# Moving VectorE's first convolution products ahead of the second tile's D folds

## The chip, the cores and the metric

The kernel runs on one core of one Trainium2 chip. The metric is the device time of one execution in microseconds, lower is better. TensorE, VectorE (DVE in the rows), ScalarE (ACT) and GpSimd (POOL) each work through their own list of instructions in order and meet at semaphores. Most loads and all transpositions by DMA are issued by SyncE (SP), in order too.

## The reference

Two layers of a gated block on x (8 x 256 x 512) with a context of the same shape. Only the first mixing step matters here:

```python
# layer 0: k = v = context, q = layernorm(x); 32 heads of 8 rows, L = 512
kv = einsum('bhil,bhjl->bijhl', k_, v_)
y = irfft(rfft(kv, 2L) * rfft(ssm_kernel, 2L))[..., :L]     # a causal convolution along l
out = y + kv * D[None, None, None, :, None]
out = einsum('bijhl,bhil->bjhl', out, q_)
x = x + tanh(g_xattn[0]) * out
# then: a ternary feed forward (hidden 1408), attention to the context with a mask,
# a 1-bit feed forward (hidden 2048) with activations quantised in groups of 64
```

## The kernel before

The convolution is done as matmuls. A tile n (NT = 16 of them) holds two heads, for all 8 batches: 128 rows of x. For each head (hh = 0, 1) the taps stand in SBUF as Toeplitz blocks, `toep[n % 2]`, 4 blocks of 128x128, loaded with an overlapping access pattern. D is folded into the taps: adding D to the tap of delay 0 adds kv * D to the convolution. The products of pairs of context rows (36 per batch and head, `kv[n % 2]`) are the moving operand; they are made by GpSimd (`pairs(n)`, three multiplications of 128x512 and one of 128x256) and ScalarE (`square(n)`). Half a tile is 10 products of blocks (`conv_part`, each recorded as two matmuls of 128x288), with results in 4 of the 8 banks of PSUM: banks 0 to 3 for hh = 0, banks 4 to 7 for hh = 1.

Per tile the engines do this.

- VectorE: `ln_sums(dve, 0, n)` (bn_stats and bn_aggr of x tile n); `products(n, hh)`, four instructions (lines 1253, 1255, 1257, 1262) that multiply the convolution's result by q and free its banks (`s_prod`); `fold_heads(n, hh)` (line 1268).
- GpSimd: `pairs(n + 1)`, `ln_root` and `conv_offset` (the reciprocal deviation and the offset from the sums), `finish_heads`, `add_result`.
- ScalarE: `join_q(n + 1)`, `square(n + 1)`, `norm_q(n + 2)` (line 1026, normalises x), `split_q(n + 2)` (line 992, parts the result into two 16-bit planes), from n = 2 `copy_result(n - 2)` (line 1033), and then pieces of the weights of the next stage.
- SP: for each n, loads of x and context and weights, then `turn_q_planes(n + 2)` (line 371, a DMA transposition of the planes, which waits for split_q), then `load_toeplitz(n + 2)` (line 359). `join_q` (line 1003) waits for the transposition to land.
- TensorE: `conv(n)`: half 0, then from n = 2 `turn_result(n - 2)` into bank 5, then half 1 in the order of blocks lo = 2, 3, 0, 1; ahead of lo = 1, which writes bank 5, it waits for `copy_result(n - 2)`.

The first tiles are special. Tile 0's and tile 1's Toeplitz blocks come straight from the input without D, and VectorE adds D on the diagonal (`fold_first_d`, line 1451, four instructions in all). Those of tiles 2 to 15 come from `kpad`, a copy of the taps in memory: VectorE adds D to the taps (line 1479, 32x1 elements), and SP then stores them (line 456). Tiles 0 and 1 of q are turned by TensorE (`turn_q`) and copied by ScalarE (`copy_q`, lines 981 and 983), the later ones by DMA. `s_first` counts the first pairs (2) and the four folds; fold_first_d(0, 1), the fourth count, comes before everything that the change touches.

In the kernel before VectorE's list begins so: first pairs, fold (0, 0), sums of x tile 0, fold (0, 1), sums of x tile 1, and then the part that the change moves. Line 1479 is the taps' add:

```python
                dve.wait_ge(s_tp[1], 16)
                fold_first_d(1, 0)
                fold_first_d(1, 1)
                dve.wait_ge(s_kin, 32)
                nc.vector.tensor_tensor(kp_sb[:, P - 1:P], kp_sb[:, P - 1:P], d_sb[:, :], ALU.add).then_inc(s_dadd, 1)
                dve.wait_ge(s_xl[2], 16)
                ln_sums(dve, 0, 2)
                for n in range(NT):
                    products(n, 0)
```

Of the kernel before, what the change touches and what calls it, by code (L numbers as in the profile page):

```python
# [5 lines left out]
ALU = mybir.AluOpType  # L6
# [8 lines left out]
P = 128  # L15
# [9 lines left out]
def at(v, off, dims):  # L25
    return bass.AP(v.tensor, v.offset + off, [v.ap[0]] + dims)


def flamingo_two_layers(nc, xc, cx, ctxt_in, ctx_in, mask, g_xattn, g_ffn, taps_in, dskip, a_w, b_w, out):
# [30 lines left out]
    with ExitStack() as ctx:  # L60
        def sb(name, shape, dt=F32):
            return ctx.enter_context(nc.sbuf_tensor(name, shape, dt))

        def sem(name):
            return ctx.enter_context(nc.semaphore(name))
# [20 lines left out]
        d_sb = sb("d_sb", [H, 1])  # L86
# [14 lines left out]
        def view(off, shape, dt=F32):  # L101
            n = 1
            for s in shape:
                n *= s
            words = n if dt == F32 else n // 2
            v = arena[:, off:off + words]
            if dt != F32:
                v = v.bitcast(dt)
            if len(shape) == 1:
                return v  # L110
            names = "abcd"[:len(shape)]
            return v.rearrange(f"p ({' '.join(names)}) -> p {' '.join(names)}", **dict(zip(names, shape)))
# [3 lines left out]
        kp_sb = view(R_A, [TAP])[0:H, :]  # L116
# [53 lines left out]
        def bank(i):  # L170
            return psum[:, i, :]
# [10 lines left out]
        s_kin = sem("taps_and_d_loaded")  # L182
        s_dadd = sem("d_folded")
        s_tfirst = sem("first_toeplitz_and_d_loaded")
        s_first = sem("first_pairs_and_d_added")
# [3 lines left out]
        s_xl = [sem(f"x_loaded{i}") for i in range(NT)]  # L189
        s_cx = [sem(f"context_loaded{i}") for i in range(2)]  # L190
        s_tp = [sem(f"toeplitz_loaded{i}") for i in range(2)]
# [87 lines left out]
        def ln_sums(dve, stage, n):  # L279
            nc.vector.bn_stats(ln_bn[:, stage, n % 2, :], x_sb[:, n, :]).then_inc(s_ln[stage], 1)  # L280
            dve.wait_ge(s_ln[stage], 2 * n + 1)
            nc.vector.bn_aggr(ln_ag[:, stage, n, :], ln_bn[:, stage, n % 2, :]).then_inc(s_ln[stage], 1)
# [56 lines left out]
        with nc.Block() as block:  # L339
# [371 lines left out]
            def _(pe):  # L711
# [6 lines left out]
                def turn_result(n, to, freed):  # L718
                    pe.wait_ge(s_res, 2 * n + 2)
                    pe.wait_ge(s_prod, freed)  # L720
                    for lb in range(LB):
                        last = nc.tensor.transpose(bank4(to)[:, lb, :], res[n % 3][:, lb, :], ident[:, :])  # L722
                    last.then_inc(s_rt, 1)
# [6 lines left out]
                def conv_block(n, hh, lo):  # L730
                    for li in range(lo + 1):
                        last = conv_part(n, hh, lo, li)
                    return last
# [33 lines left out]
                def conv(n):  # L767
                    pe.wait_ge(s_kv, n + 2)
                    pe.wait_ge(s_sq, n + 2)
                    if n == 1:  # L770
                        pe.wait_ge(s_first, 6)
                    else:
                        pe.wait_ge(s_tp[n % 2], 16 * (n // 2 + 1))
                    pe.wait_ge(s_prod, 2 * n - 1)
                    for lo in CONV_ORDER:
                        last = conv_block(n, 0, lo)
                    last.then_inc(s_y, 1)
                    pe.wait_ge(s_prod, 2 * n)
                    if n >= 2:
                        turn_result(n - 2, 5, 2 * n)  # L780
                    if n in TOT_STEP:
                        w = TOT_STEP[n]
                        pe.wait_ge(s_red, w + 1)
                        nc.tensor.matmul(bank(4)[:, w:w + 1], ones[:, :], tot[:, w:w + 1], start=True, stop=True
                                         ).then_inc(s_tot, 1)
                    for lo in CONV_ORDER:
                        if n in TOT_STEP and lo == 0:
                            pe.wait_ge(s_mean, 2 * TOT_STEP[n] + 1)
                        if n >= 2 and lo == 1:
                            pe.wait_ge(s_re, n - 1)  # L790
                        last = conv_block(n, 1, lo)
                    last.then_inc(s_y, 1)
# [450 lines left out]
            def _(dve):  # L1243
                def products(n, hh):
                    dve.wait_ge(s_y, 2 * n + hh + 1)
                    dve.wait_ge(s_qc, n + 1)
                    if n >= 2:
                        dve.wait_ge(s_res, 2 * n - 3 + hh)
                    y = psum[:, 4 * hh:4 * hh + 4, :].rearrange("p l c -> p (l c)")
                    q = q_ext[n % 3][:, hh, :]  # L1250
                    pr = prod[n % 2][hh]
                    rows = LB * B
                    nc.vector.tensor_tensor(at(pr, 0, [[SLOTS, rows], [E, 4], [1, E]]), at(y, 0, [[64, rows], [1, 32]]),  # L1253
                                            at(q, 0, [[EX, rows], [1, 4], [1, E]]), ALU.mult)
                    nc.vector.tensor_tensor(at(y, NP, [[64, rows], [E, 3], [1, E]]), at(y, E, [[64, rows], [E, 3], [1, E]]),
                                            at(q, 0, [[EX, rows], [0, 3], [1, E]]), ALU.mult)
                    nc.vector.tensor_tensor(at(pr, 32, [[SLOTS, rows], [4, 2], [1, 4]]),
                                            at(y, 32, [[64, rows], [0, 2], [1, 4]]),
                                            at(q, 4, [[EX, rows], [4, 2], [1, 4]]), ALU.mult).then_inc(s_fold, 1)
                    dve.wait_ge(s_fold, 2 * n + hh + 1)  # L1260
                    side = at(pr, 1, [[SLOTS, rows], [9, 3], [1, E]])
                    nc.vector.tensor_tensor(side, side, at(y, NP, [[64, rows], [E, 3], [1, E]]), ALU.add).then_inc(s_prod, 1)  # L1262
# [8 lines left out]
                def a_weight_mean(w):  # L1271
                    dve.wait_ge(s_tot, w + 1)
                    nc.vector.tensor_scalar(a_mean[:, w:w + 1], bank(4)[:, w:w + 1], 1.0 / (FA * L), TINY,
                                            ALU.mult, ALU.max).then_inc(s_mean, 1)
# [174 lines left out]
                def fold_first_d(n, hh):  # L1449
                    diag = toep[n][:, hh, 0:P]  # L1450
                    nc.vector.scalar_tensor_tensor(diag, at(ident[:, :], P - 1, [[-1, P]]),
                                                   d_first[:, n * G + hh:n * G + hh + 1], diag, ALU.mult, ALU.add
                                                   ).then_inc(s_first, 1)
# [18 lines left out]
                fold_first_d(0, 1)  # L1472
                dve.wait_ge(s_xl[1], 16)
                ln_sums(dve, 0, 1)
                dve.wait_ge(s_tp[1], 16)
                fold_first_d(1, 0)
                fold_first_d(1, 1)
                dve.wait_ge(s_kin, 32)
                nc.vector.tensor_tensor(kp_sb[:, P - 1:P], kp_sb[:, P - 1:P], d_sb[:, :], ALU.add).then_inc(s_dadd, 1)
                dve.wait_ge(s_xl[2], 16)  # L1480
                ln_sums(dve, 0, 2)
                for n in range(NT):
                    products(n, 0)
                    if n in TOT_STEP:
                        a_weight_mean(TOT_STEP[n])
                    fold_heads(n, 0)
                    if n in TOT_STEP:
                        w = TOT_STEP[n]
                        dve.wait_ge(s_mean, 2 * w + 1)
                        nc.vector.reciprocal(a_inv[:, w:w + 1], a_mean[:, w:w + 1]).then_inc(s_mean, 1)  # L1490
                    if n + 3 < NT:
                        dve.wait_ge(s_xl[n + 3], 16)
                        ln_sums(dve, 0, n + 3)
                    products(n, 1)
                    if NT - 3 <= n < NT - 1:
                        a_scale_x(n + 3 - NT)
                    if NT - 4 <= n < NT - 1:
                        a_stats(n + 4 - NT)
                    if n == max(TOT_STEP) + 1:
                        dve.wait_ge(s_tanh, 1)  # L1500
                        nc.vector.tensor_tensor(a_down[:, :], a_mean[:, 2:3], gates[:, 2:3], ALU.mult).then_inc(s_tanh, 1)
                    if n + 1 in TOT_STEP:
                        w = TOT_STEP[n + 1]
                        dve.wait_ge(s_wa, 4 * w + 4)
                        nc.vector.tensor_reduce(tot[:, w:w + 1], a_abs[:, w, :], AX.X, ALU.add).then_inc(s_red, 1)
                    if n < NT - 1:
                        fold_heads(n, 1)
# [170 lines left out]
```

## Time and profile before

| | |
|---|---|
| median of 3 runs | 692.79 us (692.38 to 692.96) |
| the profiled execution | 692.67 us |
| its span | 690.8 us |
| TensorE busy | 682.7 us, 99% of the span |
| VectorE busy | 581.0 us, 84% |
| ScalarE busy | 410.3 us, 59% |
| GpSimd busy | 294.7 us, 43% |
| mean granted TensorE clock | 0.998 |

The span is the stretch from the first to the last instruction of the profiled execution; the execution's own time is 1.9 us longer. The times in rows count from the start of the span. An engine's busy share is a mean over all stages; the convolution takes the first 171 us of the span.

### The profile page before, as it was taken

How to read it: one execution, taken by the hardware profiler on the slowest of the kernel's cores; microseconds unless marked ns; L12 is line 12 of the kernel's file. 1: busy time of each engine (PE TensorE's matmuls, PEld its weight loads, DVE VectorE, ACT ScalarE, POOL GpSimd, SP SyncE). 2: the span in 40 equal slices, each digit the busy share in tenths (PEclk: the TensorE clock that was granted, in tenths of full speed). 3: DMA queues.
4: the chain of work that ended last, by engine and by line, in shares of the span. 5: the costliest groups of instructions: out<-in, count | busy, mean ns of one | idle time of the engine just before them, and what ended most of it. 6: DMA issues, size and time to landing. Idle time of an engine off the chain costs nothing.

```text
span 690.8 us, 9572 instructions
## 1 busy us (share of the span) xinstructions
PE 682.7 (99%) x3162; PEld 389.0 (56%) x3162; DVE 581.0 (84%) x1054; ACT 410.3 (59%) x630; POOL 294.7 (43%) x455
## 2 busy tenths in 40 slices
PE   9999999999999999999999999999999999999997
PEld 7777777777444444577744444444444444444445
DVE  5998999999998998658957889988898888898891
ACT  3689898857779898657677344423434423434440
POOL 6799999999755554537401431111110011110000
PEclk9999999999999999999999999999999999999999
DMA  8995674653478789897040243353332233342244
GB/s 297 243 299 187 220 194 131 154 150 102 127 159 194 180 179 205 226 360 277 19 134 17 61 107 77 76 93 92 76 92 39 68 92 92 78 77 61 62 69 114
DMA packets 155376, 94.64 MB, mean 137 GB/s; under 512 B 133824, under 2 KB 134336, under 8 KB 155328
## 3 DMA queue, kind: packets, MB, share of 16 engines
q1 hardware_dynamic: 153600, 90.02, 51.4%
q0 software_dynamic: 1200, 3.93, 1.7%
q8 instruction: 25, 0.41, 0.3%
q14 instruction: 23, 0.19, 0.1%
q10 hardware_dynamic: 528, 0.09, 0.1%
HBM read 53.04 MB, written 8.47 MB: 89 GB/s over the span
## 4 chain that ended last, share of the span: by engine, by line
PE 87%; DVE 6%; POOL 3%; DMA 2%; ACT 1%; issue 1%; SPq 0%; POOLq 0%
PE psum L877 29%; PE psum L726 16%; PE psum L909 15%; PE psum L804 11%; PE psum L816 5%; PE psum L860 4%; PE psum L838 4%; DMA phase_space<-in_taps 1%; PE psum L893 1%; PE psum L827 1%; POOL phase_space L576 1%; PE psum L722 1%; DVE phase_space L1253 1%; DVE phase_space L1426 1%; DVE phase_space L1359 1%
## 5 line engine op out<-in xcount | busy, mean ns | idle before, releaser
L877 PE MATMUL psum<-phase_space 128*128 128x512 f16 x1024 | 223.8, 379 | 0.1
L877 PEld LDWEIGHTS psum<-phase_space 128*128 128x128 f16 x1024 | 99.9, 98 | 122.3 <-issue 1.7
L726 PE MATMUL psum<-phase_space 128*128 128x288 f32 x640 | 158.8, 407 | 1.4 <-DVE phase_space L1262 1.4
L726 PEld LDWEIGHTS psum<-phase_space 128*128 128x128 f32 x640 | 120.4, 191 | 33.6 <-issue 1.8
L705 POOL DMA_DIRECT2D out<-x_sb x15 | 9.3, 620 | 234.7 <-DVE x_sb L1435 234.7
L909 PE MATMUL psum<-phase_space 128*128 128x512 f16 x480 | 105.7, 379 | 0.0
L1200 ACT ACTIVATE phase_space<-psum,b_scalars 128x512 f32<-128x512 f32 x64 | 43.4, 681 | 75.3 <-PE psum L877 75.2
L1206 ACT ACTIVATE phase_space<-phase_space,magic 128x1024 f32<-128x1024 f32 x32 | 36.5, 1148 | 77.3 <-DVE phase_space L1419 77.3
L804 PE MATMUL psum<-phase_space 128*128 128x512 bf16 (+1 forms) x384 | 78.9, 362 | 0.2 <-DVE phase_space L1262 0.2
L909 PEld LDWEIGHTS psum<-phase_space 128*128 128x128 f16 x480 | 46.9, 98 | 56.7
L1404 DVE SCALAR_TENSOR_TENSOR phase_space<-psum,b_scalars,phase_space 128x512 f32<-128x512 f32 x64 | 47.7, 748 | 28.5 <-ACT phase_space L1200 28.4
L804 PEld LDWEIGHTS psum<-phase_space 128*128 128x128 bf16 x384 | 37.4, 98 | 40.2 <-DVE phase_space L1262 0.7
L576 POOL TENSOR_TENSOR phase_space<-phase_space 128x512 f32<-128x512 f32 x45 | 52.4, 1190 | 0.0
L1359 DVE TENSOR_REDUCE phase_space<-phase_space 128x8 f32<-128x512 f32 (+1 forms) x32 | 47.4, 1480 | 0.5
L280 DVE BATCH_NORM_STATS2 ln_bn<-x_sb 128x6 f32<-128x512 f32 x64 | 43.5, 679 | 2.1 <-DMA x_sb<-x_between 1.7
L1253 DVE TENSOR_TENSOR phase_space<-psum,phase_space 128x1024 f32<-128x1024 f32 x32 | 39.1, 1221 | 6.6 <-PE psum L726 6.4
L300 POOL TENSOR_SCALAR phase_space<-x_sb,ln_nm,ln_rs 128x512 f32<-128x512 f32 x48 | 37.8, 788 | 13.1 <-POOL ln_rs L295 6.0
L816 PE MATMUL psum<-phase_space 128*128 128x512 bf16 x176 | 40.6, 379 | 0.9 <-issue 0.6
L1066 ACT ACTIVATE phase_space<-psum,a_scalars 128x512 f32<-128x512 f32 (+1 forms) x48 | 30.8, 642 | 14.1 <-PE psum L804 13.1
L307 POOL TENSOR_TENSOR phase_space<-phase_space 128x512 f16<-128x512 f32 x12 | 13.8, 1179 | 59.4 <-ACT phase_space L1212 59.4
L1426 DVE SCALAR_TENSOR_TENSOR phase_space<-phase_space 128x1024 f32<-128x1024 f32 x32 | 37.8, 1224 | 1.3
L1301 DVE SCALAR_TENSOR_TENSOR phase_space<-psum,a_scalars,phase_space 128x512 f32<-128x512 f32 (+1 forms) x48 | 33.2, 697 | 5.9 <-ACT phase_space L1066 4.9
(123 smaller groups left out, 1070.9 us busy)
## 6 DMA issues: line engine op xcount, KB each, us to landing
phase_space<-in_L_weights SPq DMA_DIRECT2D x24, 512.0 KB, 6.0
phase_space<-in_L_weights SPq DMA_DIRECT2D x12, 704.0 KB, 7.2
phase_space<-kpad SPq DMA_DIRECT2D x14, 512.0 KB, 4.3
phase_space<-in_context_heads SPq DMA_DIRECT2D x15, 384.0 KB, 5.0
x_sb<-in_x_tiles SPq DMA_DIRECT2D x16, 256.0 KB, 4.8
phase_space<-in_context_turned SPq DMA_DIRECT2D x8, 512.0 KB, 5.9
x_between<-x_sb SPq DMA_DIRECT2D x16, 256.0 KB
x_sb<-x_between SPq DMA_DIRECT2D x16, 256.0 KB, 7.0
```

Source lines behind the costliest of these rows:

```text
L280: nc.vector.bn_stats(ln_bn[:, stage, n % 2, :], x_sb[:, n, :]).then_inc(s_ln[stage], 1)
L576: nc.gpsimd.tensor_tensor(at(kv_k, d * E, [[NP, rows], [1, E]]), at(cx_sb[k], 0, [[EX, rows], [1, E]]), at(cx_sb[k], d, [[EX, rows], [1, E ...
L726: return nc.tensor.matmul(at(bank(4 * hh + lo), 0, [[64, B], [1, NP]]), toep[n % 2][:, hh, (lo - li) * P:(lo - li + 1) * P], kv[n % 2][:, ...
L804: last = nc.tensor.matmul(bank(UPA[c][part])[:, 0:w], fa_qT[t % 4][:, kk, :], a_wT[part][:, kk, c0:c0 + w], start=(kk == 0), stop=(kk == L ...
L816: last = nc.tensor.matmul(bank(6 + t % 2), fa_hT[t % 2][:, c, :], a_wT[2][:, c, :], start=(c == 0), stop=(c == JA - 1))
L877: last = nc.tensor.matmul(bank(2 * (m % 3) + w), fb_qT[n % 2][:, kk % 2, kk // 2, :], b_wT[w][:, kk // 2, c * 512:(c + 1) * 512], start=(k ...
L909: last = nc.tensor.matmul(bank(6 + k), fb_hT[k][:, part, c, :], b_wT[2][:, c, :], start=(c == 0 and part == 0), stop=(c == JB - 1 and part ...
L1200: nc.scalar.activation(fb_s[m % 2], bank(2 * (m % 3)), ACT.Silu, scale=fb_sm[:, n % 4, 2:3]).then_inc(g_si, 1)
L1253: nc.vector.tensor_tensor(at(pr, 0, [[SLOTS, rows], [E, 4], [1, E]]), at(y, 0, [[64, rows], [1, 32]]), at(q, 0, [[EX, rows], [1, 4], [1, E ...
L1359: nc.vector.tensor_reduce(gx[:, 0, :], grouped(src), AX.X, ALU.max, apply_absolute_value=True).then_inc(s_steps, 1)
L1404: nc.vector.scalar_tensor_tensor(fb_h[n % 2][:, c * 512:(c + 1) * 512], bank(2 * (m % 3) + 1), fb_sm[:, n % 4, 3:4], fb_s[m % 2], ALU.mult ...
L1426: nc.vector.scalar_tensor_tensor(grouped(fb_t[k][:, cols]), grouped(fb_t[k][:, cols]), MAGIC, spread(fb_gh[k][:, 3, gr], NGH // 2), ALU.su ...
```

## The change

VectorE's products(0, 0) are put ahead of the two folds of tile 1, the taps' add and the sums of x tile 2. TensorE's wait for the folds of tile 1 is split: half 0 waits for the fifth count of s_first, half 1 for the sixth.

```diff
@@ conv(n), TensorE
                     if n == 1:
-                        pe.wait_ge(s_first, 6)
+                        pe.wait_ge(s_first, 5)
                     else:
                         pe.wait_ge(s_tp[n % 2], 16 * (n // 2 + 1))
                     pe.wait_ge(s_prod, 2 * n - 1)
@@
                     last.then_inc(s_y, 1)
                     pe.wait_ge(s_prod, 2 * n)
+                    if n == 1:
+                        pe.wait_ge(s_first, 6)
                     if n >= 2:
                         turn_result(n - 2, 5, 2 * n)
@@ VectorE
                 ln_sums(dve, 0, 1)
-                dve.wait_ge(s_tp[1], 16)
-                fold_first_d(1, 0)
-                fold_first_d(1, 1)
-                dve.wait_ge(s_kin, 32)
-                nc.vector.tensor_tensor(kp_sb[:, P - 1:P], kp_sb[:, P - 1:P], d_sb[:, :], ALU.add).then_inc(s_dadd, 1)
-                dve.wait_ge(s_xl[2], 16)
-                ln_sums(dve, 0, 2)
                 for n in range(NT):
                     products(n, 0)
+                    if n == 0:
+                        dve.wait_ge(s_tp[1], 16)
+                        fold_first_d(1, 0)
+                        fold_first_d(1, 1)
+                        dve.wait_ge(s_kin, 32)
+                        nc.vector.tensor_tensor(kp_sb[:, P - 1:P], kp_sb[:, P - 1:P], d_sb[:, :], ALU.add).then_inc(s_dadd, 1)
+                        dve.wait_ge(s_xl[2], 16)
+                        ln_sums(dve, 0, 2)
```

## Rows read from the trace of the kernel before

**Rows 1.** The page's head and its first part: busy us, share, instructions

```profile
span 690.8 us, 9572 instructions
PE 682.7 (99%) x3162; PEld 389.0 (56%) x3162; DVE 581.0 (84%) x1054; ACT 410.3 (59%) x630; POOL 294.7 (43%) x455
```

**Rows 2.** TensorE's waits: line waited for, total us, times, longest us

```profile
PE psum L726 <- DVE phase_space L1262: 1.4, 1, 1.4
...
PE psum L816 <- issue: 0.6, 1, 0.6
```

**Rows 3.** The chain that ended last, first 75 us: start us, us, what

```profile
11.41 1.72 DVE phase_space L1451 x2
...
18.39 14.79 PE psum L726 x60
...
33.62 9.90 PE psum L726 x40
...
54.31 9.70 PE psum L726 x40
```

**Rows 4.** TensorE's timeline, end of tile 0: start us, us, what

```profile
13.92 3.08 PE L726 MATMUL psum<-phase_space 128*128 128x288 f32 x12
```

**Rows 5.** VectorE's timeline, 8 to 24 us

```profile
8.23 0.32 DVE L1451 SCALAR_TENSOR_TENSOR phase_space<-ident,d_first,phase_space 128x128 f32<-128x128 f32 x1
...
13.05 1.06 DVE L1479 TENSOR_TENSOR phase_space<-phase_space,d_sb 32x1 f32<-32x1 f32 x1
14.05 0.67 DVE L280 BATCH_NORM_STATS2 ln_bn<-x_sb 128x6 f32<-128x512 f32 x1
...
14.86 1.21 DVE L1253 TENSOR_TENSOR phase_space<-psum,phase_space 128x1024 f32<-128x1024 f32 x1
...
17.29 0.95 DVE L1262 TENSOR_TENSOR phase_space<-phase_space,psum 128x768 f32<-128x768 f32 x1
18.28 0.69 DVE L1268 TENSOR_TENSOR phase_space<-phase_space 128x512 f32<-128x512 f32 x1
...
19.71 1.20 DVE L1253 TENSOR_TENSOR phase_space<-psum,phase_space 128x1024 f32<-128x1024 f32 x1
...
22.14 0.95 DVE L1262 TENSOR_TENSOR phase_space<-phase_space,psum 128x768 f32<-128x768 f32 x1
```

**Rows 6.** GpSimd's timeline: pairs(1)

```profile
10.90 3.21 POOL L576 TENSOR_TENSOR phase_space<-phase_space 128x512 f32<-128x512 f32 x3
```

**Rows 7.** ScalarE's timeline, 12 to 45 us

```profile
12.24 0.38 ACT L983 ACTIVATE phase_space<-psum 128x256 f32<-128x256 f32 x1
...
16.25 0.81 ACT L1026 ACTIVATE phase_space<-x_sb,ln_off,ln_rs 128x512 f32<-128x512 f32 x1 [0.74 <-POOL ln_off L584]
...
23.21 2.10 ACT L1003 ACTIVATE phase_space<-phase_space 128x512 uint16<-128x512 uint16 x4 [4.87 <-DMA phase_space<-phase_space]
...
36.71 0.67 ACT L1033 ACTIVATE phase_space<-psum,gates 128x512 f32<-128x512 f32 x1
...
40.52 2.08 ACT L1003 ACTIVATE phase_space<-phase_space 128x512 uint16<-128x512 uint16 x4 [0.42 <-DMA phase_space<-phase_space]
...
44.86 0.67 ACT L1033 ACTIVATE phase_space<-psum,gates 128x512 f32<-128x512 f32 x1
```

**Rows 8.** SyncE's queue, 18 to 28 us

```profile
18.31 1.35 SPq L371 DMA_TRANSPOSE phase_space<-phase_space  x1
19.77 1.83 SPq L359 DMA_DIRECT2D phase_space<-kpad  x1
...
27.72 1.24 SPq L371 DMA_TRANSPOSE phase_space<-phase_space  x1
```

**Rows 9.** DMA issues from 19 to 21 us: KB each, median us to landing

```profile
phase_space<-kpad SPq DMA_DIRECT2D x1, 512.0 KB, 6.2
phase_space<-phase_space SPq DMA_TRANSPOSE x1, 4.8
```

**Rows 10.** TensorE's weight loads, 30 to 48 us

```profile
37.42 5.63 PEld L726 LDWEIGHTS psum<-phase_space 128*128 128x128 f32 x24 [0.38 <-ACT phase_space L1033]
```

**Rows 11.** Windows: us, busy (instructions) by engine, granted clock, DMA share, GB/s

```profile
17.30:18.40 1.10, 0.01 (x1) 0.04 (x1) 1.07 (x2) 1.04 (x3) 0.00 (x0) 1.00 0.03 12
...
685.00:690.80 5.80, 1.45 (x14) 1.05 (x11) 0.48 (x1) 0.00 (x0) 0.00 (x0) 0.81 0.07 23
```

## The prediction

> **What bounds the kernel now.** I read the page's head first: the span is 690.8 us and TensorE is busy for 682.7 us of it [rows 1]. So almost any time that the kernel could gain is a gap on TensorE, and any new gap there is lost for good unless a later gap takes it up. The waits of TensorE say where the gaps are: one of 1.4 us, released by VectorE's line 1262, is the only one of more than 1 us once the convolution has begun [rows 2]. The chain of work that ended last leads through it. In time order it has the two folds of D into tile 1's Toeplitz blocks at 11.41, and further on 60 matmuls that start at 18.39 and run without a break for 14.79 us [rows 3]. TensorE's own timeline gives the gap's left edge: the last 12 matmuls of tile 0 start at 13.92 and end near 17.0 [rows 4]. TensorE then idles until 18.39 for products(0, 0), which frees banks 0 to 3.
>
> VectorE's timeline shows why these products are late. Their four instructions run from 14.86 to 18.24 (17.29 + 0.95) [rows 5]. Ahead of them stand the folds, the taps' add at 13.05, which takes 1.06 us for 32x1 elements, and the sums of x tile 2 at 14.05. The short jobs are long because GpSimd's pairs(1) run beside them, three multiplications from 10.90 to 14.11 [rows 6]: the add ends just as they do, while a fold with GpSimd at small jobs took 0.32 us at 8.23 [rows 5]. The products' inputs are there earlier. The last part of copy_q(0) on ScalarE ends at 12.24 + 0.38 = 12.62 [rows 7], and the first half of tile 0's convolution is done before that.
>
> **What the change moves.** No operation is added or removed. Four products (3.38 us) pass ahead of two folds, the taps' add with its store on SP's queue, and ln_sums(0, 2). TensorE's wait for six counts of s_first becomes five, with the sixth ahead of tile 1's second half.
>
> First the intended side. Products(0, 0) start at about 12.7 instead of 14.86 and end at 12.7 + 3.38 = 16.1. Fold(1, 0) ends at 16.1 + 0.05 + 0.32, about 16.45. Both are ahead of 17.0, where TensorE is free, so the 1.39 us gap goes and tile 1 starts near 16.95.
>
> Next, what is late. VectorE now does the folds, 0.3 us each in sequence, from 16.15 to 16.75. The uncontended taps' add has no row: it lies between nothing and the 1.06 us seen beside GpSimd [rows 5]. GpSimd has finished pairs(1) by then and waits for the very sums that follow, so I take 0.1 us. The bn_stats of x tile 2 then start at 16.8 instead of 14.05: late by **2.75 us**. By the ends (products at 12.62, both folds in 0.5, add at nothing: 16.5; everything as I take it and the add at 1.06: 17.75) it is 2.45 to 3.7 us. The rule for these short jobs is in the Trainium skill, "SBUF — State Buffer", section "SBUF: two separate sides": VectorE with two SBUF inputs and GpSimd take one port pair in turn, each for a whole instruction. By it the add costs nothing extra once GpSimd is idle, and by the 1.06 us of the row it would cost 0.96 us more; the add's end at GpSimd's end agrees with the rule.
>
> VectorE's next job for TensorE is late too. The sums of tile 2 took 0.81 us from start to next start (14.05 to 14.86), and from fold_heads(0, 0) at 18.28 over the sums of tile 3 to products(0, 1) at 19.71 it was 1.43 us [rows 5]. So products(0, 1) start at 16.8 + 0.81 + 1.43 = 19.05 and end 3.38 later at 22.45. TensorE reaches that point at 16.95 + 4.93 = 21.9 (a half tile is 20 of the 60 matmuls, 14.79 / 3) [rows 3]. So 0.7 us come back as a wait there: tile 1's second half starts at about 22.6 (0.15 after the products, as at 18.39) instead of 18.39 + 4.93 = 23.3, a lead of 0.7 us.
>
> Now who waits for x tile 2. The queue is GpSimd (rstd and offset), then ScalarE's norm_q(2) at 16.25 and split_q(2), then on SP the transposition of its planes at 18.31, and behind it in the same queue the Toeplitz load of tile 2 at 19.77 [rows 7, 8]. Norm_q(2) waited for that input (0.74 us idle). SP has nothing to do meanwhile, and the DMA engines are nearly idle then (share 0.03 from 17.3 to 18.4 [rows 11]), so each of these moves by the full 2.75 us. The kpad store moves from 14.14 by about as much and lands before it is wanted. The Toeplitz load took 6.2 us to land and the transposition 4.8 [rows 9]. The load lands at 19.77 + 6.2 + 2.75 = 28.7. TensorE wants it at 22.6 + 4.93 = 27.5 and starts tile 2 at about 28.8 instead of 28.25, after a wait of 1.3 us: already 0.55 us behind the kernel before.
>
> The decisive one is further along. ScalarE's join_q(2) at 23.21 sat idle for 4.87 us until the transposition landed, and everything ScalarE does afterwards is in order behind it: square(2), norm_q(3), split_q(3). SP's transposition of tile 3 at 27.72 waits for that split; join_q(3) waits for it to land; square(3), norm_q(4), split_q(4) and copy_result(0) at 36.71 follow without a pause [rows 7, 8]. This is a rigid chain: nowhere in it is TensorE waited for. TensorE needs copy_result(0) before block lo = 1 of tile 2's second half, since that frees bank 5. It had to wait for it in the kernel before already: the weight load at 37.42 sat 0.38 us, released by L1033 [rows 10], and the 40 matmuls there took 9.90 us instead of the 9.70 of a later tile [rows 3]. There is no slack left in front of this point. With the chain late by 2.75, the weight load comes at 37.42 + 2.75 = 40.2. Only the 0.55 us of these 2.75, and the 0.2 us of the old wait, are already there when TensorE arrives, so the new gap is 2.75 - 0.55 + 0.2 = 2.4 us, and it swallows lead and lag alike.
>
> From there on the stream of TensorE is solid, and all other engines are late by the same amount, so that their distances to it are as before. (The next copy_result, at 44.86, was limited by its own chain with over 2 us in hand before TensorE wanted it, about 47.9, and keeps them; join_q(4) at 40.52 idled 0.42 us for its transfer.) [rows 7] No large wait later on is there to absorb the shift.
>
> **The sum.** -1.4 (gap at 17.0) + 0.7 (wait for products(0, 1)) + 1.3 (wait for tile 2's Toeplitz blocks) + 2.4 - 0.2 (the wait for copy_result(0), new less old) = 2.8: but for rounding, the end is late by the 2.75 us of x tile 2. The profiled execution took 692.67 us, of which 690.8 are span; with 2.75 that is 695.4. The median before is 692.79, 0.12 above, which gives **695.5 us**, 0.4% slower. A measurement of this kernel tells about 0.2% (1.4 us) from no change.
>
> **Rivals.** *A, the gap is simply saved* (the other side): TensorE starts tile 1 1.39 us earlier and keeps that: 691.4 us. It needs the three later gates to have over 1.4 us in hand. For it speaks that the gap is the only large one; against it that products(0, 1) ended at 22.14 + 0.95 = 23.09 [rows 5], only 0.2 us before TensorE wanted them, and copy_result(0) after that. It decides if copy_result(0) starts at 36.71 - 1.4 = 35.3 or earlier. Chance 0.07.
>
> *B, VectorE's next product is the only limit:* a lead of 0.7 us is kept, 692.1 us. It needs x tile 2 to be late by nothing that matters. *C, the Toeplitz load limits and copy_result(0) does not* (a faster transfer takes up two microseconds of ScalarE's chain): 0.55 us, 693.3 us. For both speaks that ScalarE has idle time: 4.87 us ahead of join_q(2). Against both, this idle time is spent waiting for the late transfer itself. Together 0.15.
>
> *D, the clock.* TensorE's granted clock stayed at 1.00 (2.4 GHz) over the 1.1 us that hold the old gap, while the 5.8 us that hold the idle end show 0.81, a mean of the two levels [rows 11]. The new gap of 2.4 us is longer than the old one, with two of 0.7 and 1.3 us ahead of it. If the clock fell to 1.2 GHz for the half tile behind it, this would take twice its 4.93 us: 695.5 + 4.9 = 700.4 us. The Trainium skill, "TensorE: Matmul & The Clock Gate", section "Part 1: The HAM clock gate", says that an idle TensorE drops to the half rate; that the idle end shows a lower clock agrees. Chance 0.04, since the old gap did nothing.
>
> **How the numbers follow.** The forecast case has 0.74, with its own range 695.1 to 696.5 from the ends 2.45 and 3.7 above. A range from 692.6 to 696.4 takes in C and most of the forecast and leaves out A, D and nearly all of B. Faster by over 0.2%: A and a small part of B, 0.09. Within 0.2%: B and C, 0.14. Slower: forecast and D, 0.77.
>
> **What the profile after should show.** Right: L1253 starting near 12.7, the four products done at 16.1; folds of 0.32 us; no gap at 17.0; TensorE waiting for L1262 until about 22.6; the transposition at 21.1 and the Toeplitz load at 22.5 on SP; join_q(2) at 26.0; copy_result(0) at 39.4 with TensorE waiting about 2.4 us for it. Wrong, if the transposition lands much faster than in 4.8 us, if copy_result(0) comes before 38, or if the shift at 54 us is not the shift at the end.

## The result, and the profile after

The changed kernel takes 694.21 us (median of 18 runs), the kernel before 692.74 (18 runs): a ratio of 1.0024, with a 95% interval from 1.0018 to 1.0031. It is slower, by 1.5 us where 2.75 were forecast. Its 18 executions fall in two groups: 14 took 693.82 to 694.64 us, four took 695.62 to 695.91; the 18 of the kernel before lie between 692.38 and 693.21. One execution of all those in this document, of the experiment e9, ran at a mean granted clock of 0.851 and took 797.66 us; it is left out. In the changed kernel products(n, hh) are lines 1255 to 1264 and fold_heads is line 1270; copy_q is at 983 and 985, norm_q at 1028, join_q at 1005 and copy_result at 1035. Times of a row can differ by up to half a microsecond between executions of one kernel: the folds of tile 1, which wait for the load of their taps, started at 11.41 in one execution of the kernel before and at 11.77 in another (e8).

TensorE's waits in the profile after, to be set against [rows 2]:

```profile
PE psum L726 <- ACT phase_space L1035: 1.8, 1, 1.8
...
PE psum L726 <- DVE phase_space L1264: 0.4, 1, 0.4
```

The wait of 1.4 us for VectorE has become 0.4, and there is a new one of 1.8 us for copy_result(0). VectorE's timeline, which answers to [rows 5], shows the intended side:

```profile
12.71 1.22 DVE L1255 TENSOR_TENSOR phase_space<-psum,phase_space 128x1024 f32<-128x1024 f32 x1 [3.11 <-ACT phase_space L985]
...
15.17 0.95 DVE L1264 TENSOR_TENSOR phase_space<-phase_space,psum 128x768 f32<-128x768 f32 x1
16.04 0.61 DVE L1453 SCALAR_TENSOR_TENSOR phase_space<-ident,d_first,phase_space 128x128 f32<-128x128 f32 x2
16.56 0.14 DVE L1484 TENSOR_TENSOR phase_space<-phase_space,d_sb 32x1 f32<-32x1 f32 x1
16.63 0.68 DVE L280 BATCH_NORM_STATS2 ln_bn<-x_sb 128x6 f32<-128x512 f32 x1
...
21.27 0.95 DVE L1264 TENSOR_TENSOR phase_space<-phase_space,psum 128x768 f32<-128x768 f32 x1
```

The first products start as soon as copy_q(0) has ended and are done at 16.12. The two folds take 0.61 us together and the taps' add 0.14, against 1.72 [rows 3] and 1.06 [rows 5] beside GpSimd's pairs(1). The sums of x tile 2 start at 16.63 instead of 14.05, and products(0, 1) end at 22.22.

What hangs on x tile 2, on GpSimd, on ScalarE (to [rows 7]) and in SyncE's queue (to [rows 8]):

```profile
17.61 0.54 POOL L289 TENSOR_SCALAR ln_ve<-ln_ag 128x1 f32<-128x1 f32 x1 [2.92 <-DVE ln_ag L282]
```

```profile
19.19 0.81 ACT L1028 ACTIVATE phase_space<-x_sb,ln_off,ln_rs 128x512 f32<-128x512 f32 x1 [3.68 <-POOL ln_off L584]
...
24.23 2.09 ACT L1005 ACTIVATE phase_space<-phase_space 128x512 uint16<-128x512 uint16 x4 [2.96 <-DMA phase_space<-phase_space]
...
37.96 0.67 ACT L1035 ACTIVATE phase_space<-psum,gates 128x512 f32<-128x512 f32 x1
```

```profile
21.24 1.36 SPq L371 DMA_TRANSPOSE phase_space<-phase_space  x1
22.71 0.51 SPq L359 DMA_DIRECT2D phase_space<-kpad  x1
...
28.73 1.24 SPq L371 DMA_TRANSPOSE phase_space<-phase_space  x1
```

Norm_q(2) is 2.94 us late, the transposition 2.93. But join_q(2) is late by 1.02 only. The DMA view of these two issues, to [rows 9], has the reason (median us from issue to landing at the end of the row):

```profile
phase_space<-kpad SPq DMA_DIRECT2D x1, 512.0 KB, 4.5
phase_space<-phase_space SPq DMA_TRANSPOSE x1, 2.9
```

The transposition landed in 2.9 us instead of 4.8, the Toeplitz load in 4.5 instead of 6.2. From there the chain goes on as rigidly as forecast: copy_result(0) is 1.25 us late. TensorE's weight loads show the three places where it waits:

```profile
22.28 4.66 PEld L726 LDWEIGHTS psum<-phase_space 128*128 128x128 f32 x20 [0.89 <-DVE phase_space L1264]
27.47 4.66 PEld L726 LDWEIGHTS psum<-phase_space 128*128 128x128 f32 x20 [0.54 <-issue]
...
38.68 5.63 PEld L726 LDWEIGHTS psum<-phase_space 128*128 128x128 f32 x24 [2.22 <-ACT phase_space L1035]
```

The first two waits are short: 0.4 us for products(0, 1), and 0.54 us between weight loads at 27.47, right after the Toeplitz load landed at 22.71 + 4.5 = 27.2. The last row answers to [rows 10]: 38.68 instead of 37.42, 1.26 us late. Up to there TensorE was ahead (its turn_result(0) started at 32.43, before at 33.02). From there on it is behind by what the chain is late, to the end: the span is 692.1 us, 1.3 more. The clock stayed up over the new gap (stretch and its length, then busy us and instructions of TensorE, its weight loads, VectorE, ScalarE and GpSimd, then the granted clock, 1.00 in both, the DMA share and GB/s):

```profile
36.50:38.70 2.20, 0.44 (x3) 0.02 (x1) 1.05 (x3) 2.17 (x5) 1.68 (x4) 1.00 0.99 415
38.70:44.60 5.90, 5.90 (x24) 4.59 (x25) 4.17 (x6) 5.89 (x10) 5.82 (x7) 1.00 0.90 248
```

### The profile page after: what moved, and what is told of

Read it like the earlier page. It is cut to its first block, busy times and chain, and to the rows that moved or that the text cites. A ratio compares the mean times of both kernels' runs of the same rounds, so it can differ in the third digit from the quotient of the medians.

```text
span 692.1 us, 9573 instructions
## 1 busy us (share of the span) xinstructions
PE 683.1 (99%) x3162; PEld 388.7 (56%) x3162; DVE 578.4 (84%) x1054; ACT 410.4 (59%) x630; POOL 295.1 (43%) x455
## 4 chain that ended last, share of the span: by engine, by line
PE 84%; DVE 5%; POOL 3%; ACT 2%; issue 1%; DMA 1%; POOLq 0%; ACTq 0%
PE psum L879 29%; PE psum L911 15%; PE psum L726 14%; PE psum L806 11%; PE psum L818 5%; PE psum L862 4%; PE psum L840 4%; PE psum L895 1%; PE psum L829 1%; POOL phase_space L576 1%; PE psum L722 1%; DVE phase_space L1428 1%; DVE phase_space L1361 1%; DVE phase_space L1255 1%; DMA phase_space<-phase_space 1%
## 5 line engine op out<-in xcount | busy, mean ns | idle before, releaser
L726 PEld LDWEIGHTS psum<-phase_space 128*128 128x128 f32 x640 | 120.0, 190 | 35.3 <-ACT phase_space L1035 2.2
```

Source lines behind the costliest of these rows:

```text
L726: return nc.tensor.matmul(at(bank(4 * hh + lo), 0, [[64, B], [1, NP]]), toep[n % 2][:, hh, (lo - li) * P:(lo - li + 1) * P], kv[n % 2][:, ...
```

## The experiments

Three theories were put against each other. Theory 1: the loss is x tile 2's chain, which ends at copy_result(0). Theory 2: it is the late taps' add with the kpad store and the Toeplitz load behind it. Theory 3: it is the new order of VectorE and TensorE itself.

**Sums of x tile 2 first.** On the changed kernel:

```diff
                 ln_sums(dve, 0, 1)
+                dve.wait_ge(s_xl[2], 16)
+                ln_sums(dve, 0, 2)
                 for n in range(NT):
                     products(n, 0)
...
-                        dve.wait_ge(s_xl[2], 16)
-                        ln_sums(dve, 0, 2)
```

> The changed kernel, but the sums of x tile 2 stand ahead of products(0, 0), where VectorE idled for 3.1 us; the two folds and the taps' add stay behind the products. Theory 1 (the loss is x tile 2's chain, which ends at copy_result(0)): norm_q(2) is back near 16.0, the Toeplitz load and copy_result(0) are back at or before their times in the kernel before (36.7), the loss of 1.5 us is gone. If the transposition lands in 4.8 us the time is 692.5 to 692.8 (TensorE still waits for copy_result(0)), if it lands in 2.9 us the wait is gone too and 691.2 to 691.6 remains. Theory 2 (the loss comes from the late folds, taps' add and kpad store, and the Toeplitz load behind them): the time stays at 694.2. Theory 3 (VectorE's later products are the limit): products(0, 1) end at about 21.4 instead of 22.2, 0.8 us are gained, 693.4.

Measured: 691.94 us, ratio 0.9989 to the kernel before (0.9980 to 0.9998). The whole loss is gone and a gain of 0.8 us is there, with folds, taps' add and kpad store as late as in the changed kernel (store at 17.13, there at 16.73). So these are not the loss. The Toeplitz load, the other half of theory 2, is early again here (20.21), as it stands behind the transposition in SyncE's queue; it is settled by e3 below. The rows of e1 on VectorE, ScalarE and TensorE's weight loads:

```profile
12.31 0.69 DVE L280 BATCH_NORM_STATS2 ln_bn<-x_sb 128x6 f32<-128x512 f32 x1 [2.44 <-DMA x_sb<-in_x_tiles]
```

```profile
16.32 0.81 ACT L1028 ACTIVATE phase_space<-x_sb,ln_off,ln_rs 128x512 f32<-128x512 f32 x1 [0.69 <-POOL ln_off L584]
...
21.54 2.10 ACT L1005 ACTIVATE phase_space<-phase_space 128x512 uint16<-128x512 uint16 x4 [3.13 <-DMA phase_space<-phase_space]
...
35.48 0.67 ACT L1035 ACTIVATE phase_space<-psum,gates 128x512 f32<-128x512 f32 x1
```

```profile
36.20 5.63 PEld L726 LDWEIGHTS psum<-phase_space 128*128 128x128 f32 x24 [0.48 <-ACT phase_space L1035]
```

The transposition landed in 3.1 us here, so the chain was 1.2 us earlier at copy_result(0) than in the kernel before, and TensorE still waited for it. The gain is what the chain allowed, not the 1.4 us of the gap. (The profiled execution, 691.58 us, was the fastest of the 11.) One thing was not seen ahead: x tile 2 had only landed at 12.31, so the sums pushed the products to 13.14.

**The sums late, all else as before.** On the kernel before:

```diff
                 nc.vector.tensor_tensor(kp_sb[:, P - 1:P], ...).then_inc(s_dadd, 1)
-                dve.wait_ge(s_xl[2], 16)
-                ln_sums(dve, 0, 2)
                 for n in range(NT):
                     products(n, 0)
+                    if n == 0:
+                        dve.wait_ge(s_xl[2], 16)
+                        ln_sums(dve, 0, 2)
```

> The kernel before, with the sums of x tile 2 alone moved behind products(0, 0); folds and taps' add stay where they were. Theory 1: products(0, 0) run from 14.1 to 17.45, the gap on TensorE shrinks to 0.65 us, the sums start at 17.5, 3.4 us later than before, and norm_q(2) near 19.9 instead of 16.25. With a transposition that lands in 4.8 us the time is 692.7 + 3.5 = 696.2, with 2.9 us 694.4. Theory 2 (late folds and taps' add cost the time): no loss, the 0.8 us of the gap are gained, 691.9.

Measured: 695.07 us, ratio 1.0034 (1.0021 to 1.0046). It is slower than the changed kernel, though taps' add and kpad store are where they were (store at 14.25). Norm_q(2) starts at 20.02, the transposition lands in 2.9 us and copy_result(0) starts at 38.81, 2.1 us late; 692.77 + 2.1 = 694.9, 0.2 us less than measured. The 694.4 of the expectation left out that the second transposition took 4.8 us instead of 4.6 and that norm_q(2) was 3.8 us late instead of 3.5.

**copy_result(0) earlier.** Three kernels have this edit on ScalarE: the changed kernel with it (e3), the changed kernel with it and the sums first (e4), and the kernel before with it (e5).

```diff
                     if n + 1 < NT:
                         square(n + 1)
+                    if n == 2:
+                        copy_result(0, 5)
                     if n + 2 < NT:
                         norm_q(n + 2)
...
-                    if n >= 2:
+                    if n >= 3:
                         copy_result(n - 2, 5)
```

> The changed kernel, with ScalarE's copy_result(0) moved two instructions groups ahead, in front of norm_q(4) and split_q(4). Theory 1 (the wait for copy_result(0) is what sets the loss): it starts at about 35.6 instead of 38.0, TensorE's wait of 1.8 us there is gone, and TensorE keeps the lead of 0.55 us that it has after tile 2's first half: 692.2, or with a transposition that lands in 4.8 us about 693.2. Rival (the wait is only moved, some later gate of tile 3 or 4 binds, since norm_q(4) and its transposition are 0.7 us later still): 694.0 or more.

Measured: 692.65 us, ratio 0.9997 (0.9988 to 1.0006). TensorE's wait for copy_result(0) fell from 1.8 to 0.2 us, and the loss of 1.5 us with it; no later gate took its place. The Toeplitz load was as late as in the changed kernel (23.19, there 22.71), so it is not the loss either: theory 2 is out, and theory 1 holds. In the profiled execution ScalarE's chain was 0.5 us later than in the changed kernel's from its start (norm_q(2) at 19.67), which is why 0.2 us of the wait remained and 692.2 was not reached.

> Both edits: the sums of x tile 2 ahead of products(0, 0), and copy_result(0) ahead of norm_q(4). Theory 1: the gap of 1.4 us at 17 is gone and nothing takes it back, nor the 0.2 us wait for copy_result(0): no gap on TensorE between 11 us and the end of the convolution, 691.1, the best kernel so far. Rival (TensorE's stream is held by transfers or by VectorE all the same): 692.5 or more.

Measured: **691.04 us**, ratio 0.9976 (0.9967 to 0.9984). It beats both kernels, by 1.7 and 3.2 us. TensorE's waits over the whole kernel:

```profile
PE psum L738 <- POOL ones L634: 1.0, 1, 1.0
PE psum L818 <- issue: 0.6, 1, 0.6
PE psum L818 <- DMA phase_space<-phase_space: 0.5, 1, 0.5
PE psum L806 <- DVE phase_space L1266: 0.2, 1, 0.2
```

None of these lines belongs to the convolution, whose matmuls are line 726. (Line 738 stands ahead of it, 806 and 818 are of later stages; the 0.2 us is the first matmul of the next stage, which waits for the last products, line 1266 here.) The gap at 17 us is gone, there is no wait for copy_result(0), and nothing took the gain back.

> The kernel before, with copy_result(0) moved ahead of norm_q(4). Theory 1: only the old wait of 0.2 us for it goes, 692.55. It also shows how much of the best kernel so far (691.04) is due to this edit alone. Rival: this edit is where that kernel's whole gain of 1.7 us comes from: 691.1.

Measured: 692.71 us, ratio 0.9997 (0.9988 to 1.0006), not to be told from the kernel before. So e4's gain is not this edit's alone; it needs the gap closed, and the gap's 1.4 us need this edit: without it 0.8 us came through.

**The chain late, VectorE and TensorE untouched.** On the kernel before, copies of x tile 2 were added on ScalarE ahead of norm_q(2), which then overwrites what they wrote; there were 2, 3 and 5 of them (e6, e7, e9).

```diff
                         act.wait_ge(s_xt, n - 1)
+                    if n == 2:
+                        for i in range(2):      # 3 in e7, 5 in e9
+                            nc.scalar.activation(xh_c[n % 2], x_sb[:, n, :], ACT.Copy).then_inc(s_late, 1)
+                            act.wait_ge(s_late, i + 1)
                     nc.scalar.activation(xh_c[n % 2], x_sb[:, n, :], ACT.Identity, ...
```

> The kernel before, VectorE and TensorE untouched, with two added copies of x tile 2 on ScalarE ahead of norm_q(2): the chain alone is late, by some 1.7 us. Theory 1: the time follows the chain, as far as the transposition's landing does: with 4.8 us to landing 694.4, with 2.9 us the lateness is made up and it is 692.6. Theory 3 (VectorE's and TensorE's own new order cost the time): 692.8 in any case.

> As the last, with three added copies: the chain is late by some 2.6 us, as in the changed kernel, while TensorE keeps its gap of 1.4 us. Theory 1: with 2.9 us to landing the time is that of the changed kernel less 0.3, near 693.9, though VectorE does nothing differently; with 4.8 us it is 695.3. Theory 3: 692.8.

> As e7, with five added copies of x tile 2 on ScalarE: norm_q(2) starts about 3.3 us late, near 19.5, and the transposition is issued near 21.6, as in the changed kernel (21.24). VectorE and TensorE are those of the kernel before, with the gap of 1.4 us at 17. Theory 1: the transposition lands in 2.9 us, copy_result(0) is 1.3 to 1.7 us late, and the time is 694.2 to 694.5, the changed kernel's. Theory 3 (VectorE's or TensorE's new order costs the time): 692.8.

Measured: 692.71 us (0.9991 to 1.0009), 693.22 us (1.0007, 0.9998 to 1.0016) and 694.71 us (1.0027, 1.0016 to 1.0038). The last is the changed kernel's loss and a little more (and 0.2 us above the range expected), with VectorE and the first wait of TensorE as before. Theory 3 is out. The rows of e9, TensorE's waits first and then ScalarE (in e9 the products end with line 1267, and copy_result is line 1038):

```profile
PE psum L727 <- ACT phase_space L1038: 1.7, 1, 1.7
PE psum L727 <- DVE phase_space L1267: 1.2, 1, 1.2
```

```profile
16.47 3.28 ACT L1029 ACTIVATE phase_space<-x_sb 128x512 f32<-128x512 f32 x5 [0.57 <-POOL ln_off L585]
...
24.79 2.10 ACT L1004 ACTIVATE phase_space<-phase_space 128x512 uint16<-128x512 uint16 x4 [2.91 <-DMA phase_space<-phase_space]
...
38.71 0.67 ACT L1038 ACTIVATE phase_space<-psum,gates 128x512 f32<-128x512 f32 x1
```

Both gaps stand side by side here, the old one and the changed kernel's. In e7 norm_q(2) was 2.0 us late and not the 2.6 expected (a copy takes 0.65 us), the transposition landed in 2.8 us, join_q(2) was back at 23.24 (before: 23.21) and copy_result(0) came 0.36 us late: 692.8 + 0.4 = 693.2. In e6 norm_q(2) was 1.5 us late and the median did not move; its profile fell on the slowest of its executions (693.51 us), in which the second transposition took 5.3 us and copy_result(0) came 0.6 us late. In e9 norm_q(2) was 3.5 us late and the time rose by 1.9. So the first 1.5 to 1.9 us by which this chain is late cost next to nothing, because the first transposition then lands sooner by as much, and what is beyond costs about its full length.

**Both kernels again.** The kernel before (e8) and the changed kernel (e10), without an edit.

> The kernel before, unchanged, for a second profile. If the 4.8 us from issue to landing of the first transposition belong to this kernel (its place right behind other transfers), they come again; if they are chance, 2.9 us are as likely. The time is 692.8 either way, since a transposition that lands earlier saves only the 0.2 us of the wait for copy_result(0).

> The changed kernel, unchanged. Of its first 18 executions 14 took 693.8 to 694.6 us and 4 took 695.6 to 695.9. Theory 1 for the four: their first transposition landed in 4.8 us, as in the kernel before, which by the sum is 692.8 + 2.9 = 695.7. If a profile falls on such an execution, join_q(2) starts near 26.1 instead of 24.2. Otherwise again about one execution in five lies near 695.7.

Measured: 692.77 us, and 694.26 us (ratio 1.0022, 1.0013 to 1.0031). The kernel before had the 4.8 us again:

```profile
phase_space<-phase_space SPq DMA_TRANSPOSE x1, 4.8
```

The changed kernel had 2.9 again. One of its 11 executions took 695.89 us, the others 693.89 to 694.61. No profile fell on such an execution, so that their first transposition took 4.8 us is argued from the sum only (692.7 + 2.9 = 695.6) and not shown; what sets these five executions (with the four above) apart stays open.

## Why the prediction was right, and where it was off

The direction and the path were forecast: the kernel is slower, by way of x tile 2's chain and copy_result(0). The size was not. The time of 694.21 us lies outside the forecast case's own range (695.1 to 696.5) and inside the stated one only because that was stretched down to 692.6 to take in rival C; that it fell inside is in part luck. Two of its own signs of being wrong came true: the transposition landed much faster than in 4.8 us, and copy_result(0) came before 38 (37.96). The third did not: the shift at 54 us (53.71 to 54.96) is the shift at the end. (A slip in the working: the lower end 695.1 is counted from 692.67, the upper end 696.5 from 692.79.)

*The gap closes, and products(0, 1) are late.* Right: products from 12.71 to 16.12 (forecast 12.7 to 16.1); tile 1's first half starts without a gap; its second half at 22.28 (22.6), after a wait of 0.4 us (0.7).

*x tile 2 is late by 2.75 us.* Right in size: 2.58 at bn_stats, 2.94 at norm_q(2). The taps' add, taken at 0.1 us with up to 1.06 as the other end, took 0.14. The 0.36 us between came from GpSimd. Its first small job took 0.54 us instead of 0.19, and it ended 0.05 us after VectorE's fold_heads did (17.61 + 0.54 = 18.15, and 17.44 + 0.66 = 18.10). The same 0.54 us, with the same 0.05, is in e2, e3 and e10, where fold_heads runs beside this job too; in e1 and e4, where it doesn't, the job took 0.19. The forecast had counted what GpSimd does to VectorE and not the reverse. The rule of the port pair in the Trainium skill ("SBUF — State Buffer", section "SBUF: two separate sides") works both ways, and these rows agree with it; no run here was made to test it.

*The Toeplitz load holds tile 2 until 28.8.* Wrong: it landed at 22.71 + 4.5 = 27.2, and tile 2 started at 27.47, still ahead of the kernel before. At turn_result(0) TensorE was 0.6 us ahead (32.43 for 33.02) where 0.55 us behind was forecast.

*copy_result(0) decides, with no slack.* Right in place and kind, shown three ways: by taking the lateness away (e1), by taking the wait away (e3), by making the chain late alone (e9). The step that failed is "so each of these moves by the full 2.75 us": the term was right up to the issue of the transposition (2.93) and wrong at its landing, 4.8 us in the kernel before and 2.9 after, so that join_q(2) moved by 1.02. What TensorE lost was 2.94 - 1.9 + 0.2 (the next transposition took 4.8 instead of 4.6) = 1.24, measured 1.26 at the weight load. The prediction took one duration of a transfer as fixed, although the profile of before has transpositions of this size that landed in 2.8 us; case C had named this as a chance, but ended it at the Toeplitz load. The prediction's ground, DMA engines nearly idle, was read from 17.3 to 18.4, ahead of the issue; from 20 to 22 us, while the transposition was under way, the trace of before has a DMA share of 1.28 with only 25 GB/s moved. What the transposition met there, from 19.5 on, is told in the last section.

*A* needed copy_result(0) at 35.3 or earlier, which the change alone did not give (37.96): e1 shows how near that is (35.48), and e4 has it. *D* did not come: the granted clock was 1.00 over the gap and behind it.

## What to carry to other kernels

When an engine's queue is reordered to close a gap on the bound engine, follow what was moved back through every queue to the next place where the bound engine waits, even 20 us later: here a gap of 1.4 us was exchanged for one of 1.8. A moved piece should be parted by who waits for whom: the folds and the taps' add could go behind the products at no cost, the sums could not, and they would have fitted into VectorE's idle time ahead of them. And a wait of 0.2 us marks a place that turns into time all lateness that reaches it: relieve it first, even if doing so alone gains nothing (e5). Before a transfer's duration is carried over to another moment, look at what ran beside it: the same transposition took 4.8 us at one moment and 2.9 at another.

## What the runs showed of the hardware

The first DMA transposition of the planes (issued by SyncE, 128x512 of 16 bit in two planes) did not take the same time from issue to landing in all kernels. The DMA packets in the traces show what goes with it. The transposition is moved in 1024 packets of 256 bytes, the first of them about 1.3 us after the issue. In every kernel there is one transfer of 16 KB near it that no line of the program issues; the profile lists it as queue 8, kind "instruction", so it is called a fetch here. By time of issue, the packets' columns in us from the start of the span:

| kernel | issued at, us | first packet | fetch, from to | landed after, us |
|---|---|---|---|---|
| e4 | 17.93 | 19.2 | 18.3 to 19.6 | 3.5 |
| before | 18.31 | 19.6 | 19.5 to 21.2 | 4.8 |
| e1 | 18.37 | 19.7 | 18.7 to 19.6 | 3.1 |
| e8 (before again) | 18.48 | 19.8 | 19.8 to 21.4 | 4.8 |
| e5 | 18.56 | 19.8 | 19.9 to 20.9 | 4.0 |
| e6 | 19.83 | 21.1 | 19.8 to 21.2 | 3.1 |
| e7 | 20.29 | 21.6 | 19.5 to 20.7 | 2.8 |
| after | 21.24 | 22.5 | 18.4 to 19.5 | 2.9 |
| e10 (after again) | 21.30 | 22.6 | 18.5 to 19.5 | 2.9 |
| e3 | 21.73 | 23.0 | 18.9 to 19.9 | 2.9 |
| e9 | 21.85 | 23.1 | 19.8 to 21.0 | 2.8 |
| e2 | 22.08 | 23.4 | 18.9 to 19.8 | 2.9 |

Where the fetch had ended 0.8 us or more before the first packet, the transposition landed in 2.8 to 2.9 us, six times of six. Where they met, or missed each other by 0.05 us (e1), it took longer, and the longer the more they overlapped: 3.1 us for e1 and e6, 3.5 for e4, 4.0 for e5, 4.8 for the kernel before twice. In the kernel before the packets stop halfway. These are GB/s in slices of 0.125 us over the 5 us from the issue (the window from 18.3, and for the changed kernel from 21.2), with the row of the fetch in the first window:

```profile
GB/s 0 0 0 0 0 0 0 0 0 131 61 238 274 272 176 14 0 0 0 0 0 0 0 6 8 10 8 10 10 143 285 291 328 175 279 344 360 295 295 164
q8 instruction: 1, 0.02, 2.1%
...
GB/s 0 0 0 0 0 0 0 0 0 0 20 197 289 287 289 293 291 289 138 6 0 115 49 49 213 295 328 393 229 213 115 279 262 279 197 197 180 213 229 295
```

The two kernels themselves have it again further on, with hardly any other transfer beside the packets. In the kernel before the transposition issued at 134.07 landed in 4.6 us with a fetch from 135.2 to 136.8, and those issued at 114.65 and 124.78 landed in 2.8 us with none; in the changed kernel 135.31 has 4.8 us with a fetch, 115.90 and 126.04 have 2.8 without.

So the 4.8 us were most likely not a property of the transposition but its meeting with the fetch, and the changed kernel parted the two: the transposition came 2.9 us later, and the fetch 1.1 us earlier (18.4 for 19.5) once tile 1 started on TensorE without its gap. (In e2, where tile 1 started at 17.68 instead of 18.39, the fetch came at 18.9.) This is read from the traces alone: no experiment moved the fetch by itself, and which engine's instructions it brings is not shown. The kpad store is not what makes the difference: it was early in e7 and e9 (2.8 us to landing) as in the kernel before (4.8). Beside weight loads transpositions took long without any fetch (4.6 us for the one issued at 27.72 in the kernel before, at a DMA share of 1.03 from 29 to 30 us), so a fetch is one cause of a late landing and not the only one.
